# Attention stage of a four-layer kernel: score units of three PSUM banks instead of two, one stream of score items, and one bank shared by means and turns

## The reference, cut to what matters

```
q = proj_h(v @ Wq.T)      # (B=2, h=16, T=2048, 16); the first entry of a head is sqrt(1 + sum of squares)
k = proj_h(v @ Wk.T)
vv = (v @ Wv.T) by heads  # (2, 16, 2048, 16)
sc = (-q0 * k0 + q[1:] . k[1:]) / 4
at = softmax(sc, axis=-1)
out = at @ vv             # then the output projection, in the next stage
```

## Time and profile before

| what | us |
|---|---|
| median of 3 runs | 2381.38 |
| the profiled execution, its own time | 2376.76 |
| its span, first to last instruction | 2375.0 |
| first to last start of an exponential of the stage (L1783) | 749.6 to 1726.8 |
| ACT busy with the 1024 exponentials | 964.3 |
| PE busy in the span | 2071.7 (87%) |
| DVE busy in the span | 1369.0 (58%) |

### The profile page before, as it was taken

How to read it: one execution, slowest core, us unless ns; L and a number is a source line. 1 busy time by engine, 2 the same in 40 slices (tenths; PEclk the granted TensorE clock), 3 DMA queues, 4 the chain that set the end, 5 groups by cost and what they waited for, 6 DMA issues and landing times. The chain is left out here.

```text
span 2375.0 us, 42994 instructions
## 1 busy us (share of the span) xinstructions
PE 2071.7 (87%) x13329; PEld 965.9 (41%) x13330; DVE 1369.0 (58%) x2970; ACT 1534.8 (65%) x2495; POOL 419.7 (18%) x394
## 2 busy tenths in 40 slices
PE   5996799950996999999999999999973499999994
PEld 3785555530661222222222222222252367676763
DVE  5566544457786444444445555554137787777773
ACT  2215433324774999999999999999964344444442
POOL 0030266642000000000000000001000033443431
PEclk9998899985996999999999999999996799999997
DMA  5001355543100000000002222222163567766774
GB/s 197 1 1 71 94 155 153 151 168 120 36 24 1 1 2 1 1 1 1 1 19 72 72 72 72 72 72 72 54 205 141 185 180 174 175 173 172 173 174 130
DMA packets 144821, 216.20 MB, mean 91 GB/s; under 512 B 13904, under 2 KB 117376, under 8 KB 144688
## 3 DMA queue, kind: packets, MB, share of 16 engines
q1 hardware_dynamic: 123696, 175.13, 23.7%
q0 software_dynamic: 20448, 37.24, 6.8%
q10 hardware_dynamic: 544, 2.10, 0.3%
HBM read 157.63 MB, written 56.66 MB: 90 GB/s over the span
## 5 line engine op out<-in xcount | busy, mean ns | idle before, releaser
L1783 ACT ACTIVATE at_pexp<-at_psS 128x1024 f32<-128x1024 f32 x1024 | 964.3, 1023 | 43.7 <-PE at_psS L1689 40.5
L1797 DVE TENSOR_REDUCE at_mx<-at_psM 128x1 f32<-128x512 f32 x474 | 327.3, 691 | 465.3 <-PE at_psM L1716 465.3
L1703 PE MATMUL at_psO<-at_pexp,at_vst 128*32 128x512 f32 x4096 | 547.0, 606 | 0.1
L1689 PE MATMUL at_psS<-l1c_QT,l1c_KT 64*128 64x512 f16 x2048 | 403.7, 387 | 14.5 <-issue 5.6
L1689 PEld LDWEIGHTS at_psS<-l1c_QT,l1c_KT 64*128 64x128 f16 x2048 | 99.6, 93 | 633.2 <-ACT at_pexp L1783 599.7
L2129 PE MATMUL ex_psH<-wide_wgu,ex_xT 128*128 x1278 | 259.5, 357 | 0.4 <-DVE ex_bias L2200 0.2
L2200 DVE SCALAR_TENSOR_TENSOR ex_bias<-ex_psH,top_w_scale,ex_bias 128x456 f32<-128x456 f32 x213 | 147.4, 692 | 75.7 <-PE ex_psH L2129 60.6
L2173 ACT ACTIVATE ex_sg<-ex_bias 128x228 f32<-128x228 f32 x213 | 83.7, 393 | 151.7 <-DVE ex_bias L2200 151.6
L1716 PE MATMUL at_psM<-at_ksumT,l1c_QT 64*128 64x512 bf16 x474 | 179.1, 378 | 0.6
L971 POOL DMA_INDIRECT ex_xg<-normed,top_tok x142 | 139.0, 979 | 202.1 <-POOLq L80 151.2
L2129 PEld LDWEIGHTS ex_psH<-wide_wgu,ex_xT 128*128 128x128 f16 x1278 | 124.3, 97 | 111.7 <-issue 3.3
(11 more groups left out here) (359 smaller groups left out, 2706.3 us busy)
## 6 DMA issues: line engine op xcount, KB each, us to landing
ex_bias<-in_L_ffn_bg SPq DMA_DIRECT2D x71, 342.0 KB, 4.7
ex_bias<-in_L_ffn_b SPq DMA_DIRECT2D x71, 342.0 KB, 5.5
ex_piece<-in_L_ffn_W SPq DMA_DIRECT2D x48, 228.0 KB, 2.6
l1c_KT<-in_L_ffn_W SPq DMA_DIRECT2D x32, 342.0 KB, 3.3
halves<-l1c_KT SPq DMA_DIRECT2D x32, 342.0 KB, 2.8
wide_wgu<-halves SPq DMA_DIRECT2D x8, 1368.0 KB
ex_b<-in_L_ffn_b SPq DMA_DIRECT2D x71, 128.0 KB, 4.5
normed<-rt_area SPq DMA_DIRECT2D x16, 512.0 KB, 2.6
```

The source lines that it names most:

```text
L1689: mm = pe.matmul(psS[:, n, hh * BANK:(hh + 1) * BANK], keys(k.KT, p)[r, kt * P:(kt + 1) * P], keys(k.QT, p)[r, c * BANK:(c + 1) * BANK], s ...
L1703: mm = pe.matmul(psO[g * VW:(g + 1) * VW, y, :], vst[:, p % 2, hh, kt, :], pexp[:, (p * ST + step) % 3 * 2 + n, hh * BANK:(hh + 1) * BANK] ...
L1783: act.activation(pexp[:, u % 6, :], psS[:, u % 2, :], ACT.Exp, scale=D ** -0.5 / (QS * QS)).then_inc(raised, 1)
L1797: dve.tensor_reduce(mx[:, n:n + 1], psM[:, :], AX.X, ALU.max).then_inc(reduced, 1)
```

## The change

A unit becomes three items (3 banks, 1536 columns), and the ring of two units takes 6 banks. psO goes from two banks to one, and `psX` is gone: means, shift turns and out turns all use `psM`, so 6 + 1 + 1 = 8 banks. The 16 x 128 = 2048 items form one stream that runs through from pair to pair, so there are 683 units (the last has two items). Within a pair the order of items is now query half outside, key tiles inside, then the two blocks and the two heads; the heads alternate, so a unit holds a pair of items on different row halves and a third item alone. In a slot u the mean, where there is one, is of the head on the other row half than the third item, and is issued right behind it. `pexp` holds 4 units of three banks (12 as before).

A slot of PE's program is: scores of unit u, a mean if the slot has one, a product if the slot has one, a turn if the slot has one. Products still take four items each, so 512 products are spread over 683 slots, three in four slots. `value_slots()` places product n in the slot (4n+3)//3 + 2 or later, one to a slot, and the first product of a half pair at least two slots behind the last of the half before it, since they share the one psO bank. `bank_use()` places out turns two slots behind the last product of a half, keeps means out of that slot and the next, fills the other slots with the means of the next pair from five slots ahead of the pair's predecessor on, and puts the shift turn two slots behind the last of them. `bank_free()` adds the wait for the last user of `psM`.

`sum_keys` is done in four quarters. In the first pair, the shift's turn and copy come ahead of the three first means of pair 1. The diff, cut to its core:

```diff
-    UN = 2 * BANK
+    UI = 3
+    UN = UI * BANK
-    TURN = ST - 4
-    SPLIT, SR = (7, 9, 14, 16, 21, 23), 3
+    ITEMS = 4 * ST
+    NU = -(-NPAIR * ITEMS // UI)
+    PR = 4
+    SUMS = (7, 8, 11, 14)
+    SPLIT, SR = (10, 13, 19, 22, 28, 31), 3
...
-        pexp = s.sb("pexp", [P, 6, UN])
+        pexp = s.sb("pexp", [P, PR, UN])
...
-        psO = s.ps("psO", [P, 2, BANK])
+        psO = s.ps("psO", [P, BANK])
         psM = s.ps("psM", [P, BANK])
-        psX = s.ps("psX", [P, BANK])
...
+        def base(p):
+            return -(-p * ITEMS // UI)
+
+        def value_slots():
+            at, u = [], 1
+            for n in range(NPAIR * ST):
+                u = max(u + 1, (4 * n + 3) // UI + 2)
+                if n and n % KT16 == 0:
+                    u = max(u, at[-1] + 2)
+                at.append(u)
+            return at
+
+        v_slot = value_slots()
+        v_at = {u: n for n, u in enumerate(v_slot)}
+        out_at = {v_slot[n * KT16 + KT16 - 1]: (n // 2, n % 2) for n in range(2 * NPAIR)}
+
+        def bank_use():
+            turns = {u + 2: ("out", p, y) for u, (p, y) in out_at.items()}
+            taken = {u + d for u in turns for d in (0, 1)}
+            found, u = {}, 0
+            for q in range(1, NPAIR):
+                u = max(u, base(q - 1) - 5, 0)
+                left = [list(range(AHEAD // 2 if q == 1 else 0, KT16)) for _ in range(2)]
+                while left[0] or left[1]:
+                    if u not in taken:
+                        hh = 1 - u % 2
+                        hh = hh if left[hh] else 1 - hh
+                        found[u] = (q, hh, left[hh].pop(0))
+                        last = u
+                    u += 1
+                u = last + 2
+                while u in taken or u + 1 in taken:
+                    u += 1
+                assert u <= base(q) - 4
+                turns[u] = ("shift", q, 0)
+                taken |= {u, u + 1}
+            return found, turns
...
+        def bank_free(eng, u, turn):
+            if turn and u in mean_in:
+                eng.wait_ge(reduced, mean_no[mean_in[u]] + 1)
+                return
+            for v in range(u - 1, -1, -1):
+                if v in turn_in:
+                    eng.wait_ge(x_free, x_use[turn_in[v]] + 1)
+                    return
+                if v in mean_in:
+                    eng.wait_ge(reduced, mean_no[mean_in[v]] + 1)
+                    return
+            eng.wait_ge(x_free, 1)
...
-                def scores(p, step, n):
-                    kt, c = step // 2, (step % 2) * 2 + n
-                    u = (p * ST + step) * 2 + n
-                    pe.wait_ge(raised, u + 1)
-                    for hh in range(2):
+                def scores(u):
+                    if u >= 2:
+                        pe.wait_ge(raised, u - 1)
+                    for at in range(u * UI, min((u + 1) * UI, NPAIR * ITEMS)):
+                        p, n = at // ITEMS, at % ITEMS
+                        if n == 0:
+                            pe.wait_ge(shift_in, 32 * (p + 1))
+                        kt, c, hh = n // 4 % KT16, n // (4 * KT16) * 2 + n % 4 // 2, n % 2
...
-                for p in range(NPAIR):
-                    pe.wait_ge(shift_in, 32 * (p + 1))
-                    for step in range(ST):
-                        scores(p, step, 0)
-                        if step >= 2:
-                            weigh(p, step - 2)
-                        elif p:
-                            weigh(p - 1, ST - 2 + step)
-                        scores(p, step, 1)
...
+                for u in range(NU + 5):
+                    if u < NU:
+                        scores(u)
+                    if u in mean_in:
+                        means(u, *mean_in[u])
+                    if u in v_at:
+                        weigh(v_at[u])
+                    if u in turn_in:
+                        kind, p, y = turn_in[u]
+                        if kind == "out":
+                            turn_out(u, p, y)
+                        else:
+                            turn_shift(u, p)
...
-                for u in range(NPAIR * ST * 2):
+                for u in range(NU):
                     act.wait_ge(scored, u + 1)
-                    act.wait_ge(weighed, u + 1)
-                    act.activation(pexp[:, u % 6, :], psS[:, u % 2, :], ACT.Exp,
+                    if u >= PR:
+                        act.wait_ge(weighed, ((u - PR) * UI + UI - 1) // 4 + 1)
+                    width = min(UI, NPAIR * ITEMS - u * UI) * BANK
+                    act.activation(pexp[:, u % PR, 0:width], psS[:, u % 2, 0:width], ACT.Exp,
                                    scale=D ** -0.5 / (QS * QS)).then_inc(raised, 1)
...
-                dve.sem_inc(weighed, 6)
-                def sum_keys(p):
+                def sum_keys(p, first, last):
...
+                for u in range(NU + 5):
+                    p = min(u * UI // ITEMS, NPAIR - 1)
+                    at = u - base(p)
+                    if u in mean_in:
+                        q, hh, t = mean_in[u]
+                        reduce(q, hh, t)
+                        if u == mean_last[q]:
+                            make_shift(q)
+                    if u in out_at:
+                        take_out(*out_at[u])
+                    if at in SUMS and p + 2 < NPAIR:
+                        sum_keys(p + 2, SUMS.index(at), SUMS.index(at) + 1)
+                    if at in SPLIT and p >= HPAIR:
+                        low((p - HPAIR) * NSP + SPLIT.index(at))
+                    if u in turn_in:
+                        kind, p, y = turn_in[u]
+                        if kind == "out":
+                            divide(p, y)
+                        else:
+                            put_shift(p)
```

More of the change, by code:

```diff
@@ new lines, in attention @@
+        mean_in, turn_in = bank_use()
+        x_use = {use: n + 1 for n, (_, use) in enumerate(sorted(turn_in.items()))}
+        x_use["shift", 0, 0] = 0
+        mean_no = {use: ST + AHEAD + n for n, (_, use) in enumerate(sorted(mean_in.items()))}
+        mean_last = {q: max(u for u in mean_in if mean_in[u][0] == q) for q in range(1, NPAIR)}
+        def bank_free(eng, u, turn):
[10 more added lines that the diff above has]
+            eng.wait_ge(x_free, 1)
@@ L1590, in early @@
         def early(at):
-            return (psS[:, 0, :], psS[:, 1, :], psO[:, :, :].rearrange("p a c -> p (a c)"))[at % 3].rearrange(
+            return psS[:, :, :].rearrange("p r c -> p (r c)")[:, at % 3 * 2 * BANK:(at % 3 + 1) * 2 * BANK].rearrange(
                 "p (h c) -> p h c", h=2)
@@ L1697, in weigh @@
                     if kt == 0:
-                        if p:
-                            pe.wait_ge(o_out, 2 * (p - 1) + y + 1)
+                        if y:
+                            pe.wait_ge(o_out, y)
                         pe.wait_ge(v_ready, p + 1)
                     for g in range(4):
-                        n, hh = g // 2, g % 2
-                        mm = pe.matmul(psO[g * VW:(g + 1) * VW, y, :], vst[:, p % 2, hh, kt, :],
-                                       pexp[:, (p * ST + step) % 3 * 2 + n, hh * BANK:(hh + 1) * BANK],
+                        at = 4 * n + g
@@ L1705, in weigh @@
+                        mm = pe.matmul(psO[g * VW:(g + 1) * VW, :], vst[:, p % 2, g % 2, kt, :],
+                                       pexp[:, at // UI % PR, at % UI * BANK:(at % UI + 1) * BANK],
                                        start=(kt == 0), stop=(kt == KT16 - 1))
[L1706 to L1714, removed]
+                    mm.then_inc(weighed, 1)
@@ L1715, in means @@
+                def means(u, p, hh, t):
+                    pe.wait_ge(k_ready, 4 * (p + 1))
+                    bank_free(pe, u, False)
                     r = slice(hh * HR, (hh + 1) * HR)
@@ L1787, in _, with reduce @@
             def _(dve):
-                dve.sem_inc(weighed, 6)
-                def sum_keys(p):
+                def sum_keys(p, first, last):
+                    g = TS // GM // 4
                     with nc.allow_low_precision(reason="the shift need not be exact"):
[L1792 to L1797, removed]
+                        dve.tensor_reduce(ksumT[:, p % 2, first * g:last * g],
+                                          keys(k.KT, p)[:, first * g * GM:last * g * GM].rearrange("p (g m) -> p g m", m=GM),
+                                          AX.X, ALU.add).then_inc(k_ready, last - first)
+                def reduce(p, hh, t):
+                    dve.wait_ge(maxed, mean_no[p, hh, t] + 1)
+                    dve.tensor_reduce(mx[:, 2 * t + hh:2 * t + hh + 1], psM[:, :], AX.X, ALU.max).then_inc(reduced, 1)
                 def first_reduce(p, t):
@@ L1879, in _ @@
-                for y in range(2):
-                    take_out(NPAIR - 1, y)
-                for y in range(2):
-                    divide(NPAIR - 1, y)
+                for u in range(NU + 5):
[18 more added lines that the diff above has]
```

(1 more changed line is left out.)

87 lines of the change are left out of this document (23 added, 64 removed).

## The result

| | before | after |
|---|---|---|
| median of the runs (7 each), us | 2381.23 | 2389.37 |
| lowest to highest | 2374.56 to 2381.84 | 2383.88 to 2392.38 |
| ratio, 95% interval | | 1.0038 [1.0023, 1.0053] |
| profiled execution, its span | 2375.0 | 2390.6 |
| stage, first to last start of an exponential | 977.2 | 986.7 |

A forecast was written before the change was run, and what follows sets the result against it. ACT and PE, within 5% of each other, bound the kernel. Stage: 677 + 101 + 201 + 2 = 981, plus 2.2, 983 against 977.2 (+6); start -1.4, end -0.6; together +4: 2385.5 us, range 2350 to 2408.

The forecast's parts named there:

- free pace of 1536 columns: On ACT, distance between starts of exponentials that nothing holds: 0.915 + 0.427 = 1.342 us.
- slot with a product: On PE, scores, third item with the mean beside it, then product: 0.23 + 0.32 + 1.00 = 1.55 us.
- mean to mean at the least: Means share one bank: 0.41 to the reduction, 0.69 for it, 0.05 (from the prelude) until PE continues: 1.16 us.
- block of four with means: Four slots in the mean phases, three with products: 3 x 1.55 + 1.16 = 5.81 us, against 5.66 before.
- joints, 62 slots: Slots where half pairs meet and exponentials wait for products or turns: 43 + 30 + 28 = 101 us.
- joint with two waits (11): 11 of 31 joints, two exponentials in a row waiting for products: 1.80 and 2.14 us instead of 1.34.
- a mean's wait for the reduction: PE's mean load waiting for DVE's previous reduction: about 118 times, up to 0.7 us each, 80 us.
- first start (from ACT's table load) and end: Outside the stage: first scores 1.4 us earlier, last exponential to last division 0.6 us shorter.
- ACT pacing (1): In mean phases ACT sets the pace, blocks 5.42 to 5.45 us: about 35 us less, 2350 us; chance 0.17.
- a slot of 1.52 (2): PE's product slots take 1.52 us, perhaps with shorter release of the mean's bank: 2362 to 2374 us; chance 0.18.
- no overlap (3): On PE, third item and mean don't run side by side, 0.21 us more per mean slot: +75, 2460 us; chance 0.08.
- worse joints (4): At 31 joints each product wait also finds the next mean's reduction late, 0.5 us each: +15, 2400 us; chance 0.12.

The follow-up runs named there:

- a_act1024: Changed kernel with exponentials of 1024 instead of 1536 columns from the fifth unit on, the third item left out: stage 961.7 us, time 2363.30 us.
- a_samehalf: Changed kernel with each slot's mean on the same row half as the third score item: stage 1051.0 us, time 2451.19 us.

## Why the prediction was right, step by step

The direction was right and the size half: +4 forecast, +8 measured (by the stage and its two ends: +9.5 - 1.0 - 0.7 = +7.8). The direction was a close call, slower 0.40 against faster 0.35 in the forecast's own chances; what the experiments bear out is the path it described.

| term | forecast | measured |
|---|---|---|
| free pace of 1536 columns | 1.342 | 1.33 to 1.35 |
| length of one | 1.45 | 1.451 |
| slot with a product | 1.55 | 1.53 |
| mean to mean at the least | 1.16 | 1.28 |
| block of four with means | 5.81 | 5.87 |
| slots with means (463 of them) | 1.43 each | 669.3, 1.446 each |
| joints, 62 slots | 101 | 101.2 |
| joint with two waits (11) | 1.80, 2.14 | 1.77, 2.12 |
| other 147 slots | 201 | 200.5 |
| a mean's wait for the reduction | about 118 times, 80 us | 102 times, 97 us |
| exponentials' waits for products | 21 of 31 joints | 32 waits, 13.3 us |
| first start (from ACT's table load) and end | -1.4, -0.6 | -1.0, -0.7 |

The measured sums are those of the starts of the exponentials in the trace, behind the tenth slot. The term that was mis-sized is the one that decides: the mean's distance, 1.28 and not 1.16. Its parts were 0.41 + 0.69 + 0.05. The first is 0.44 where the mean runs beside the third score (1007.72 to 1008.16) and 0.41 only where it goes alone (1009.00 to 1009.41). The last, from the end of a reduction to the mean it releases, was taken from the prelude's load; it is 0.15 here (1008.85 to 1009.00), 0.12 to the load and 0.03 more to the matmul. The product slot was 0.02 too long, which by chance gave about half of it back.

The two programs show where the 0.15 is likely to come from; the forecast has no term for it. Cut from `means`, before and changed:

```
# before                                  # changed
if n == 0:                                pe.wait_ge(k_ready, 4 * (p + 1))
    pe.wait_ge(k_ready, p + 1)            bank_free(pe, u, False)
if p * ST + n:
    pe.wait_ge(reduced, p * ST + n)
```

The changed kernel waits for two semaphores ahead of every mean: `k_ready`, whose key sums are made a pair ahead, and the bank. The kernel before had both only for the first mean of a pair. With two waits, the one for the bank is a semaphore instruction of its own in the trace. These are its rows by line, changed kernel (L1639 is in `bank_free`), then before:

```profile
L1639 PEldq EVENT_SEMAPHORE  x474: 51/51/51, 749.9 to 1662.5; - x158
```

```profile
L1713 PEldq EVENT_SEMAPHORE  x14: 51/51/51, 800.8 to 1595.3; - x14
```

At the wait above it runs from 1008.89 to 1008.94, between the reduction's end at 1008.85 and the load at 1008.97. The load itself carries the wait for `k_ready`, so the profile finds no releaser for its idle time and writes "issue". One of the 14 waits for DVE in the kernel before, at full clock and with the wait on the load:

```profile
774.53 0.68 DVE L1797 TENSOR_REDUCE at_mx<-at_psM 128x1 f32<-128x512 f32 x1
...
775.27 0.09 PEld L1716 LDWEIGHTS at_psM<-at_ksumT,l1c_QT 64*128 64x128 f16 x1 [0.34 <-DVE at_mx L1797]
775.27 0.39 PE L1716 MATMUL at_psM<-at_ksumT,l1c_QT 64*128 64x512 bf16 x1
```

Reduction to matmul is 0.06 there, in all 14, and 0.15 in all 105 places of the changed kernel where a mean goes as soon as the reduction before it lets it (the profile puts down 102 of them as waits of the load). So the prelude's 0.05 was not a matter of its clock. That the second wait costs the 0.09 is read from the two traces; no run takes it out. If it does, 105 times 0.09 are some 9 us, an estimate, which is about all that the stage lost.

Of the rivals, ACT pacing (1) is ruled out by a_act1024 and by the two cuts of the reduction; a slot of 1.52 (2) was nearly so, 1.53, but the release was longer, not shorter; no overlap (3) is ruled out by a_samehalf; worse joints (4) by the starts. What was expected as a signature, some 118 waits for DVE of 80 us, came as 102 of "issue" and 80 for DVE, 97 us together: in the right places, fewer and longer, and under a name that I had not thought of.

What the forecast did not say: the profiled execution is 15.6 us longer, 7.3 of them behind the stage (1732.0 to 2375.0 before, 1740.3 to 2390.6 after), in work that the change does not touch. The medians show 8 in all; the span of one profile alone would have doubled the effect. Why that later work took longer in this execution is not known.

## What to carry to other kernels

When the longest engine gets a better shape, work out how late its neighbour may be: here ACT's free stage fell from 937 to 917 us, and PE, which had 5% of room, paced it. Two operations that share one buffer set a smallest distance from each other; in an uneven schedule it is the closest pair, not the average, that pays it, and everything queued behind pays with it. Where a distance is short, read every wait ahead of the instruction: one that is always passed can still put a semaphore instruction into the chain. Measure an idle engine's latency by shortening its instruction: DVE, 58% busy by the page, was worth 39 us of stage with nearly all of its reductions' length gone (0.19 us instead of 0.69).

## What the runs showed of the hardware beyond the forecast

A wait on another engine can show as "issue" on the weight load and as the true releaser only on the matmul behind it (73.5 and 23.8 us for one wait), when the load has a second wait and the first stands ahead of it as a semaphore instruction of 0.05 us. A mean beside a third score reached DVE 0.44 us behind its start, a mean alone 0.41. And ACT's pace on 1536 columns over three banks is on the line from 256 and 1024 columns (0.38 and 1.02 us): 1.451 us long, 1.33 to 1.35 apart, so no cost shows for the third bank.
